# Expert stages: exponentials and both similarities in the middle of the turn, dense products of the first half in two pieces, eight input buffers

## What is computed

```python
def _L0_ffn_ref(hidden_states, W_up, W_down, W_q, keys, down_embed, up_embed):
    ...
    q = jnp.einsum('btd,ed->bte', hidden_states, W_q)
    q = q.reshape(b, t, 2, h, n).transpose(2, 0, 1, 3, 4)
    sim = jnp.einsum('pbthn,hkpn->pbthk', q, keys)
    scores_xy, idx_xy = jax.lax.top_k(sim, K)
    ...
    all_scores = (sx[..., :, None] + sy[..., None, :]).reshape(b, t, h, K * K)
    ...
    scores, pk = jax.lax.top_k(all_scores, K)
    indices = jnp.take_along_axis(all_idx, pk, axis=-1)
    de = down_embed[indices]
    ue = up_embed[indices]
    w = jax.nn.silu(jnp.einsum('btd,bthkd->bthk', hidden_states, de) * jax.nn.softmax(scores, axis=-1))
    experts_states = jnp.einsum('bthk,bthkd->btd', w, ue)
    dense = jnp.einsum('bti,di->btd', jax.nn.silu(jnp.einsum('btd,id->bti', hidden_states, W_up)), W_down)
    return dense + experts_states
...
    x = x + 0.5 * _L0_ffn_ref(_layernorm(x, axis=-1), ...)
    x = x + _L0_attn_ref(_layernorm(x, axis=-1), ...)
    x = x + 0.5 * _L0_ffn_ref(_layernorm(x, axis=-1), ...)
    x = x + 0.5 * _L1_ffn_ref(_layernorm(x, axis=-1), ...)
    x = x + _L1_attn_ref(_layernorm(x, axis=-1), ...)
    x = x + 0.5 * _L1_ffn_ref(_layernorm(x, axis=-1), ...)
```

## Time and profile before

| | before |
|---|---|
| median of 3 runs | 4067.43 us (4067.26 to 4078.61) |
| profiled execution | 4069.94 us, span 4068.1 us |
| mean granted TensorE clock | 0.978 of full |
| busy over the span | PE 3722.0 us (91%), DVE 3259.7 (80%), ACT 2727.0 (67%), POOL 2442.6 (60%) |
| one turn of an expert stage, first mask to first mask | 33.81 us (616.35 to 650.16) |
| first and last output of the two expert stages | 80.6 and 3363.0 us |

### The profile page before, as it was taken

The page is one execution under the profiler, slowest core; times in us unless marked ns, Lnnn a source line. Parts: engine busy times, 40 slices in busy tenths (PEclk is TensorE's granted clock), DMA queues, the critical chain, the costliest instruction groups (busy, mean ns, idle before and its releaser), DMA issues. The chain is left out here.

```text
span 4068.1 us, 79094 instructions
## 1 busy us (share of the span) xinstructions
PE 3722.0 (91%) x27416; PEld 3185.4 (78%) x27416; DVE 3259.7 (80%) x7738; ACT 2727.0 (67%) x7878; POOL 2442.6 (60%) x2330
## 2 busy tenths in 40 slices
PE   6999999999969999999997799999999987999989
PEld 5777777777758888888886577777777776898878
DVE  7888888888758888888875888888888876856577
ACT  5666666666559999999995566666666646633166
POOL 6777777777555555655541677777777755612266
PEclk8999999999989999999998899999999998999999
DMA  4555555555510000000001455555555552331342
GB/s 113 110 110 109 110 110 110 109 110 109 107 49 18 12 23 18 18 23 12 23 7 40 98 109 109 109 109 110 110 110 109 109 105 89 115 111 56 122 155 90
DMA packets 190349, 343.11 MB, mean 84 GB/s; under 512 B 14816, under 2 KB 138112, under 8 KB 189952
## 3 DMA queue, kind: packets, MB, share of 16 engines
q0 software_dynamic: 55296, 201.35, 26.0%
q1 hardware_dynamic: 134656, 136.71, 10.6%
HBM read 80.06 MB, written 56.62 MB: 34 GB/s over the span
## 5 line engine op out<-in xcount | busy, mean ns | idle before, releaser
L300 POOL TENSOR_TENSOR f_grid<-f_ex 128x1024 f32<-128x1024 f32 x512 | 1003.8, 1966 | 245.3 <-DVE f_q L710 241.7
L701 DVE SCALAR_TENSOR_TENSOR f_p_u<-f_grid,f_te,f_p_dot 128x1024 f32<-128x1024 f32 x512 | 653.2, 1276 | 236.0 <-PE f_p_dot L106 235.7
L1533 ACT ACTIVATE a_ex<-a_p_s,a_mneg 128x128 f32<-128x128 f32 x2048 | 726.0, 406 | 92.4 <-DVE a_mneg L1587 92.4
L710 DVE SCALAR_TENSOR_TENSOR f_q<-f_p_u,f_rz,f_grid 128x1024 f32<-128x1024 f32 x512 | 652.0, 1274 | 4.8
L445 PE MATMUL f_p_y<-f_wdn,f_hs 128*128 128x256 f32 x2048 | 474.0, 385 | 80.1 <-ACT f_hs L555 79.0
L310 POOL DMA_DIRECT2D f_q<-f_q x384 | 350.4, 913 | 259.0 <-DMA f_q<-f_q 145.4
L1533 ACT ACTIVATION_READ_ACCUMULATOR a_ex<-a_p_s,a_mneg 128x1 f32 x2048 | 503.5, 246 | 0.0
L445 PEld LDWEIGHTS f_p_y<-f_wdn,f_hs 128*128 128x128 f32 x2048 | 382.0, 191 | 141.7 <-ACT f_hs L555 92.2
L450 PE MATMUL f_p_y<-f_eup,f_wT 128*128 128x256 f32 x2048 | 479.0, 382 | 1.2
L450 PEld LDWEIGHTS f_p_y<-f_eup,f_wT 128*128 128x128 f32 x2048 | 374.3, 190 | 68.5 <-ACT f_wT L549 25.3
L549 ACT COPY f_wT<-f_p_wT 128x512 f32<-128x512 f32 x256 | 148.5, 580 | 288.5 <-PE f_p_wT L433 288.5
(11 more groups left out here) (645 smaller groups left out, 11009.0 us busy)
## 6 DMA issues: line engine op xcount, KB each, us to landing
f_q<-f_q POOLq DMA_DIRECT2D x384, 512.0 KB, 4.6
x_f<-f_yt SPq DMA_DIRECT2D x64, 256.0 KB, 3.8
f_xt<-x SPq DMA_DIRECT2D x32, 256.0 KB, 4.1
a_xt<-x_f SPq DMA_DIRECT2D x16, 512.0 KB, 3.8
x_a<-a_yt SPq DMA_DIRECT2D x16, 512.0 KB, 2.9
f_xt<-x_a SPq DMA_DIRECT2D x32, 256.0 KB, 4.2
c_xt<-x_f SPq DMA_DIRECT2D x16, 512.0 KB, 4.7
x_c<-c_yt SPq DMA_DIRECT2D x16, 512.0 KB, 3.1
```

The source lines that it names most:

```text
L300: g_grid.mark(pool.tensor_tensor(grid[v][:, hd, :].rearrange("p (i j) -> p i j", i=XROWS), sx[:, hd, :].unsqueeze(2).to_broadcast([P, XROW ...
L701: d_mask.mark(dve.scalar_tensor_tensor(out=p_u[:], in0=grid[v][:, hd, :], scalar=te[:, v, hd, TOP - 1:TOP], in1=p_dot[:], op0=ALU.is_ge, o ...
L710: d_mul.mark(dve.scalar_tensor_tensor(out=q[v][:, hd, :], in0=p_u[:], scalar=rz[:, v, hd:hd + 1], in1=grid[v][:, hd, :], op0=ALU.mult, op1 ...
L1533: last = act.activation(ex[t.step % 2][:, i, n, :], p_s[i][:, n, :], ACT.Exp, bias=mneg[:, i, n:n + 1], accum_out=z[t.step % 2][:, i, n:n ...
```

## The change

The number of input buffers xt goes from 4 to 8 and loads are issued four turns ahead; ex has two buffers, so that the exponentials of t+2 wait only for readers of turn t. `dense` is split in two pieces of four chunks. The work of the engines is put in another order:

- PE: `turn_w(t, 0, 0)` goes behind `dots(t+1, 0)`, and with it comes the second piece of `dense(t, 0)`, then `turn_h`, then `turn_w(t, 0, 1)`. `similar(t+2, 0)` and `similar(t+2, 1)` go from around `hidden(t, 2)` to around `hidden(t, 1)`. `dense(t-1, 1)` goes behind `dots(t, 1)`.
- ACT: the exponentials go from the end of the turn to its middle, `exps(t+2, 0)` behind `back(t, 0)` and `exps(t+2, 1)` behind `turned(t-1, 1, 1)`; `third(t, 1)` now stands before `hidden(t, 2)`; `normed` is done at the end of the turn before.
- DVE: `turned(t+2)`, both `lowest(t+2, v)` and `front(t+3)` are done in half 0; `output` goes two places back.
- POOL: one `scores` stands before `summed(t-1, 1, 2)`, `root(t+3)` goes to the middle, one `summed` changes place with one `scores`.

No arithmetic instruction is added or removed.

```diff
-        xt = [m.sbuf(f"xt{k}", V, D) for k in range(4)]
+        xt = [m.sbuf(f"xt{k}", V, D) for k in range(8)]
...
-        sim, ex = (m.sbuf(k, V, 2 * HEADS * KEYS) for k in ("sim", "ex"))
+        sim = m.sbuf("sim", V, 2 * HEADS * KEYS)
+        ex = [m.sbuf(f"ex{k}", V, 2 * HEADS * KEYS) for k in range(2)]
...
+                load(first + 3)
...
-                    if (t + 3).exists(last=count):
-                        load(t + 3)
+                    if (t + 4).exists(last=count):
+                        load(t + 4)
...
+                    if after:
+                        scores(t + 1, 0, (0,))
                     if (t - 1).exists():
                         summed(t - 1, 1, 2)
                     if after:
-                        scores(t + 1, 0, (0, 1))
+                        scores(t + 1, 0, (1,))
...
                     clamps(t, 0)
+                    summed(t, 0, 1)
                     if after:
                         scores(t + 1, 0, (3,))
-                    summed(t, 0, 1)
                     tails(t, 1)
+                    if (t + 3).exists(last=count):
+                        root(t + 3)
...
+                def dense(t, v, k):
+
+                    if v == 0:
+                        a_hid.wait(pe, t, "3" if k else "1")
+                        if k == 0 and (t - 1).exists():
+                            d_out.wait(pe, t - 1, "1")
+                    elif k == 0:
                         d_out.wait(pe, t, "0")
-                    else:
-                        a_hid.wait(pe, t, "3")
-                        if (t - 1).exists():
-                            d_out.wait(pe, t - 1, "1")
-                    for e in range(EC):
+                    for e in range(k * HALF, (k + 1) * HALF):
```

The order of PE:

```diff
                 def step(t):
                     before, after, later = (t - 1).exists(), (t + 1).exists(last=count), (t + 2).exists(last=count)
                     if before:
+                        turn_w(t - 1, 0, 0)
+                        dense(t - 1, 0, 1)
+                    if later:
+                        turn_h(t + 2)
+                    if before:
                         turn_w(t - 1, 0, 1)
                     hidden(t, 0)
                     if before:
                         experts(t - 1, 0, 0)
                         experts(t - 1, 0, 1)
+                    if later:
+                        similar(t + 2, 0)
                     hidden(t, 1)
                     if before:
-                        dense(t - 1, 1)
                         turn_w(t - 1, 1, 0)
                     if later:
-                        turn_h(t + 2)
+                        similar(t + 2, 1)
                     dots(t, 1)
                     if before:
                         turn_w(t - 1, 1, 1)
+                        dense(t - 1, 1, 0)
+                        dense(t - 1, 1, 1)
                         experts(t - 1, 1, 0)
                         experts(t - 1, 1, 1)
-                    if later:
-                        similar(t + 2, 0)
                     hidden(t, 2)
-                    if later:
-                        similar(t + 2, 1)
                     hidden(t, 3)
-                    dense(t, 0)
-                    turn_w(t, 0, 0)
+                    dense(t, 0, 0)
                     if after:
                         dots(t + 1, 0)
                 turns(pe, count, unroll, step)
+                turn_w(end, 0, 0)
+                dense(end, 0, 1)
                 turn_w(end, 0, 1)
                 for k in range(2):
                     experts(end, 0, k)
-                dense(end, 1)
                 for k in range(2):
                     turn_w(end, 1, k)
+                for k in range(2):
+                    dense(end, 1, k)
                 for k in range(2):
                     experts(end, 1, k)
```

The order of ACT:

```diff
-                    if (t - 1).exists():
-                        g_grid.wait(act, t - 1, f"{v}3")
-                        d_top.wait(act, t - 1, f"maxes{v}")
+                    if (t - 2).exists():
+                        g_grid.wait(act, t - 2, f"{v}3")
+                        d_top.wait(act, t - 2, f"maxes{v}")
...
+                normed(first + 2)
...
                 def step(t):
                     before, later = (t - 1).exists(), (t + 2).exists(last=count)
                     if before:
-                        turned(t - 1, 0, 1)
-                    if later:
-                        normed(t + 2)
-                    hidden(t, 0)
-                    front(t, 0)
-                    hidden(t, 1)
-                    third(t, 0)
-                    if before:
-                        turned(t - 1, 1, 0)
-                    back(t, 0)
+                        turned(t - 1, 0, 0)
                     if later:
                         turn_h(t + 2)
                     if before:
+                        turned(t - 1, 0, 1)
+                    hidden(t, 0)
+                    front(t, 0)
+                    if later:
+                        similar(t + 2, 0)
+                    third(t, 0)
+                    hidden(t, 1)
+                    if before:
+                        turned(t - 1, 1, 0)
+                    if later:
+                        similar(t + 2, 1)
+                    back(t, 0)
+                    if later:
+                        exps(t + 2, 0)
+                    if before:
                         turned(t - 1, 1, 1)
                     if later:
-                        similar(t + 2, 0)
+                        exps(t + 2, 1)
                     front(t, 1)
+                    third(t, 1)
                     hidden(t, 2)
-                    if later:
-                        similar(t + 2, 1)
-                    third(t, 1)
                     hidden(t, 3)
                     back(t, 1)
-                    turned(t, 0, 0)
-                    if later:
-                        exps(t + 2, 0)
-                        exps(t + 2, 1)
+                    if (t + 3).exists(last=count):
+                        normed(t + 3)
```

The order of DVE:

```diff
                     for v in range(V):
                         mask(t, v, 0)
                         weigh(t, v, 0)
-                        if v and later:
+                        if v == 0 and later:
                             turned(t + 2)
                         if after:
                             maxes(t + 1, v, range(0, 3))
...
                         weigh(t, v, 1)
-                        if before:
-                            output(t - 1, v)
                         if after:
                             maxes(t + 1, v, range(5, 8))
                         mask(t, v, 2)
-                        if v and later:
-                            lowest(t + 2, 0)
                         if after:
                             maxes(t + 1, v, range(8, 10))
                         weigh(t, v, 2)
+                        if before:
+                            output(t - 1, v)
                         if after:
                             maxes(t + 1, v, range(10, 12))
                         mask(t, v, 3)
                         tail_dots(t, v)
                         weigh(t, v, 3)
+                        if v == 0 and later:
+                            lowest(t + 2, 0)
+                            lowest(t + 2, 1)
                         if after:
                             best(t + 1, v)
                             inverse(t + 1, v)
-                    if later:
-                        lowest(t + 2, 1)
-                    if (t + 3).exists(last=count):
-                        front(t + 3)
+                        if v == 0 and (t + 3).exists(last=count):
+                            front(t + 3)
```

More of the change, by code:

```diff
@@ L214, in expert_ffn @@
             m.sem(k) for k in ("s_id", "s_q", "s_e", "s_z", "s_fold", "s_ws", "s_hi", "s_lo"))
-        s_ld = [m.track(f"s_ld{k}", inc=16) for k in range(4)]
+        s_ld = [m.track(f"s_ld{k}", inc=16) for k in range(8)]
         s_st = [m.track(f"s_st{k}", inc=16) for k in range(2)]
-        norm = Norm(m, V, lambda t: xt[t.step % 4], half)
+        norm = Norm(m, V, lambda t: xt[t.step % 8], half)
         shift, a_h = m.sbuf("shift", 2, 2, V), m.track("a_h")
@@ L521, in normed @@
                     for v in range(V):
-                        last = act.activation(h[:, v, :], xt[t.step % 4][:, v, :], ACT.Identity,
+                        last = act.activation(h[:, v, :], xt[t.step % 8][:, v, :], ACT.Identity,
                                               bias=shift[:, k, 1, v:v + 1], scale=norm.rstd[:, k, v:v + 1])
@@ L618, in step @@
                     if before:
+                        turned(t - 1, 0, 1)
[13 more added lines that the diff above has]
+                    if before:
                         turned(t - 1, 1, 1)
                     if later:
-                        similar(t + 2, 0)
+                        exps(t + 2, 1)
                     front(t, 1)
+                    third(t, 1)
```

(17 more changed lines are left out.)

19 lines of the change are left out of this document (7 added, 12 removed).

## The result

| | before | after |
|---|---|---|
| median, measured side by side | 4069.14 us (4067.26 to 4078.61, 4 runs) | 4205.68 us (4198.09 to 4210.35, 4 runs) |
| profiled execution | 4069.94 us, span 4068.1 | 4207.54 us, span 4205.7 |
| mean granted TensorE clock | 0.978 | 0.952 |
| half 0, half 1 of a turn (mean of turns 1 to 28, first stage) | 15.30, 18.53 us | 18.09, 17.87 us |

The ratio is 1.033, with a 95% interval from 1.031 to 1.035. The change makes the kernel 3.3% slower; the forecast was 4218 us.

A forecast was written before the change was run, and what follows sets the result against it. A turn was taken as a ring of DVE and PE, with PE's order deciding when DVE goes on. 56 turns x (0.9 order + 1.8 clock) = 151 us more, so 4218 us for the median; range 4110 to 4290.

The forecast's parts named there:

- Half 1's path: From half 1's first mask through `third`, `hidden(t, 2)`, `hidden(t, 3)`, half of `dense` and `dots`: 16.4 us, saving 2.1.
- Half 0: First `weigh` waits 1.7 us for the second `turn_w`; DVE's own work bounds the half at 18.3 us instead of 15.3.
- The clock: PE idles 3.3 us before `hidden(t, 3)` in every turn, TensorE's clock falls behind it: 1.8 us each turn.
- The other end, 2.83: Upper price in us of one clock fall, read from turn 30; the lower end was 1.65.
- 0.83 us a tile: Clock price estimated from the skill page's loop, 26.7 us lost over 32 tiles; it would make 47 us here.
- The ends: First turn and last three turns of each stage: set at nothing, 5 us either way for each stage.
- The sum: Over 56 turns, 0.9 us of order plus 1.8 of clock each: 151 us more.
- The range that the prediction calls its own: The main forecast's range, 4165 to 4285 us, for 1.0 to 3.0 us of clock; chance 0.66.
- (1): Rival: the clock stays at full speed behind PE's wait, only the order costs; 4118 us, chance 0.12.
- (2): Rival: the clock falls but costs only 0.83 us a turn; 4164 us, chance 0.05.
- (3): Rival: half 1's last adding transfer lands late and adds 1 us to each turn; 4274 us, chance 0.08.
- (4): Rival: faster, because the first `weigh` does not wait for `turn_w`; turn 33.0 us, kernel 4022 us, chance 0.06.

The follow-up runs named there:

- PE kept busy: Changed kernel with 8 extra unread matmuls of 512 columns between `hidden(t, 2)` and `hidden(t, 3)` on PE: 4124.87 us, ratio 1.013.
- 0.74 us of work: Changed kernel with two more unread `bn_stats` on DVE, in two runs: at the end of half 0's list 4293.00 us, of half 1's 4208.43 us.
- both orders mended: Changed kernel with second `turn_w` before `dense`'s second piece and `hidden(t, 2)` before `third`: 3955.69 us; also with `front(t+3)` in half 1 and `root` later: 3972.37 us.

## Why the prediction was right

**Half 1's path.** Forecast: `hidden(t, 3)` starts 10.0 us behind the first mask, the half lasts 16.4 at full clock. Measured: 648.01 - 638.00 = 10.01, and 16.25 with PE kept busy. The swap of `third` and `hidden(t, 2)` is the costly step: undone, half 1 is 14.21, 2.0 us shorter by the order and 1.6 by the clock. One thing about the order before was read short: besides 0.91 and 1.28 us PE waited a third time in each turn, 0.53 us before `hidden(t, 3)`. No term of the sum used it.

**Half 0.** Forecast 18.3, with `weigh` waiting 1.7 and starting 3.0 us behind the mask. Measured 18.06, 1.82 and 3.11. That it is bounded by DVE is shown by 0.74 us of work: 0.64 longer in half 0, nothing in half 1. From `weigh` to the next mask DVE takes 14.95 us, where I had 15.3; this is the larger part of a small error in the sum, and half 1 at 16.25 for 16.4 is the rest. So the order costs 18.07 + 16.25 - 33.83 = 0.5 us a turn, not 0.9.

**The clock.** Forecast 3.3 us of waiting, a fall in every turn, 1.8 us each. Measured 2.77 to 3.49, a fall in all 28, 1.62 each in the mean. The end of the range that had unbroken PE work behind the wait, 1.65, was the right one: 1.4 to 1.7 us where the clock was low for 3.4 us. The other end, 2.83, was right for a low stretch of 6.8 us: 2.9 us in the three such turns of both stages. The Trainium skill (TensorE: Matmul & The Clock Gate, Part 1) says that for modeling the ramp penalty is under 1% of a typical kernel span. It says so of the ramp of a typical kernel; taken as a bound on the whole loss of a kernel that pays it in every turn, as the prediction weighed it, it does not hold: the 81 us that the filled wait gave back are 1.9% of 4205.7. The estimate of 0.83 us a tile from the figures of the same page (HAM oscillation — how this bites in real kernels) is half of the 1.62 us measured here.

**The ends.** Set at nothing, within 5 us a stage. The two halves of turn 0 took 37.2 us in both stages, for 32.1 and 32.7 before. `turned` waits there as the forecast said it might; how much of the 5 us is this wait no run tells:

```profile
start us, us, engine line op out<-in xcount [idle before <-releaser]
49.69 0.69 DVE L659 TENSOR_TENSOR f_hT2l<-f_p_sim,f_hT2h 128x512 fp32r<-128x512 f32 x1 [3.57 <-ACT f_hT2h L537]
```

The last turns take 1 to 2 us more.

**The sum.** Between the two profiled executions lie 138 us. 56 turns x (35.93 - 33.83) make 118, the two turns 0 make 10, the last turns 3, and 7 lie outside these. The forecast of 151 was 33 too high in the turns (2.7 us each for 2.1) and 20 too low outside them. That it came within 13 us of the sum is in part luck: the two errors offset. The range that the prediction calls its own has a slip too: its lower end, 4165, is 0.85 us of clock by its own sum and not 1.0, which would be 4174. Nothing hung on it.

**The rivals.** The clock did not stay (1) and its price was not 0.83 (2). The transfer did come late, `turn_w` waited up to 1.0 us for it, but taking that wait away changed nothing here (3); it cost time in one turn of the kernel with PE kept busy and in the kernels with both orders mended. `weigh` did wait (4). The buffers had no part in a turn.

**Where the gain went.** The split by itself gives 72 us. The two orders around it take it away and more: the awaited `turn_w` behind the second piece, and `third` ahead of `hidden(t, 2)`. With both mended the change is worth 2.8%. The other moves (`similar`, `dense(t-1, 1)`, the exponentials, POOL's) were not undone one by one, so how the rest of the 0.5 us divides among them is open.

## What to carry to other kernels

When a long step is split to free a path, look at what the moved piece is now ahead of: here four chunks of `dense` stood before the one group of transposes that DVE waited for, and cost 100 us, about a third of it through the clock. On an engine that feeds TensorE, the order of two short instructions decides whether TensorE waits once for long or twice for little, and the long wait is paid a second time in the clock: price both, and try a few unread matmuls in the wait to see which part is which. After mending one wait, look at the traces again: the late adding transfer cost nothing in the changed kernel and up to 2.7 us in a turn of the mended ones. When forecasting, count the first and last turns of a loop by their own rows; they held 13 of 138 us here.

## What the hardware showed

- A wait of 2.42 us on PE, with the same work behind it, was followed by the low clock in 18 of 28 turns and not in 10, in either stage. Waits of 2.77 to 3.49 us in the changed kernel were followed by it every time, but three of 3.05 us, with the other DVE work in half 0, were not. In the kernels whose usual wait there was 0.7 to 1.3 us it never fell behind that wait in turns 1 to 28; it fell once, behind a wait of 2.83 us for a transfer.
- The price is not fixed. Behind 2.8 to 3.5 us of waiting the clock was low for 3.4 us in 26 of 28 turns and cost 1.4 to 1.7 us; in the two others it was low for 6.8 us and cost 2.9. Behind 3.8 us it was low for 6.8 us, some of it lying in the wait, and cost 2.6.
- Eight matmuls of 512 columns, 2.03 us of work for nothing, bought 1.62 us in each turn. It is a measuring tool; the better cure was the order that shortens the wait.
